# Attending two chunks in a row into the two halves of one bank, and turning their sums' reciprocals together

## What is computed

```python
xq = layer_norm(x, qn_w, qn_b)
ctx = layer_norm(context, cn_w, cn_b)
q = (xq @ q_w).reshape(B, N, H, D)                # B 16, N 256, H 16, D 32
kv = (ctx @ kv_w).reshape(B, M, 2, H, D)
attn = jnp.einsum('bnhd,bmhd->bhnm', q, k) * scale
attn = jnp.where(xa_mask[:, None, :, :], neg, attn)
attn = jax.nn.softmax(attn, axis=-1)
out = jnp.einsum('bhnm,bmhd->bnhd', attn, v).reshape(B, N, C)
x = x + out @ proj_w + proj_b
```

## Time and profile before

| | us |
|---|---|
| median of 3 runs (2743.96 to 2746.96) | 2745.2 |
| the profiled execution, its own time | 2744.09 |
| its span, first to last instruction | 2742.4 |
| PE busy in the span | 2672.3 (97%) |
| DVE busy | 1952.7 (71%) |
| ACT busy | 1558.8 (57%) |
| POOL busy | 734.9 (27%) |
| mean granted PE clock | 0.995 |

### The profile page before, as it was taken

How to read it: one execution, slowest core, us unless ns; L and a number is a source line. 1 busy time by engine, 2 the same in 40 slices (tenths; PEclk the granted TensorE clock), 3 DMA queues, 4 the chain that set the end, 5 groups by cost and what they waited for, 6 DMA issues and landing times.

```text
span 2742.4 us, 68931 instructions
## 1 busy us (share of the span) xinstructions
PE 2672.3 (97%) x24032; PEld 2329.0 (85%) x24032; DVE 1952.7 (71%) x5572; ACT 1558.8 (57%) x4829; POOL 734.9 (27%) x935
## 2 busy tenths in 40 slices
PE   5999999999999999999999999999899999999997
PEld 5888888888888888888889999998788888888886
DVE  6878888887534443445388887887688888888876
ACT  5777777777211111111277777777676766767763
POOL 2333333330000000001013333333233434334343
PEclk9999999999999999999999999999999999999998
DMA  4333333342311211113021111112322212222110
GB/s 152 110 106 97 108 124 102 100 143 86 92 59 34 61 46 46 46 46 100 24 78 46 46 46 46 48 53 73 108 67 69 87 61 75 78 66 95 61 52 19
DMA packets 182230, 202.57 MB, mean 74 GB/s; under 512 B 19344, under 2 KB 109456, under 8 KB 181264
## 3 DMA queue, kind: packets, MB, share of 16 engines
q1 hardware_dynamic: 182160, 201.66, 23.3%
HBM read 137.65 MB, written 63.96 MB: 74 GB/s over the span
## 4 chain that ended last, share of the span: by engine, by line
PE 82%; DVE 8%; ACT 5%; issue 3%; POOL 1%; DMA 1%; SPq 1%; DVEq 0%; ACTq 0%; POOLq 0%
PE mask_work L172 13%; PE mlp_f L3028 13%; PE mlp_acc L3046 13%; PE causal_work L172 9%; PE cross_work L172 9%; PE mask_attended L2079 2%; PE mask_scores L2039 2%; PE mask_probsT L2060 2%; PE mask_scores L2060 2%; PE causal_scores L2039 2%; ACT cross_prob L865 2%; PE cross_probsT L2060 2%; PE causal_attended L2079 2%; PE cross_scores L2039 2%; PE causal_probsT L2060 1%
## 5 line engine op out<-in xcount | busy, mean ns | idle before, releaser
L2824 ACT ACTIVATE mlp_h<-mlp_f,mlp_b1col 128x512 f32<-128x512 f32 x128 | 88.3, 690 | 524.3 <-PE mlp_f L3028 524.3
L3028 PE MATMUL mlp_f<-mlp_xT_hi,mlp_w 128*128 128x512 f32 x1024 | 335.4, 389 | 0.0
L2929 DVE CAST mlp_hT_hi<-mlp_h 128x512 fp32r<-128x512 f32 x128 | 58.2, 454 | 369.8 <-ACT mlp_h L2824 369.7
L3046 PE MATMUL mlp_acc<-mlp_w,mlp_hT_hi 128*128 128x512 f32 x1024 | 315.2, 389 | 0.0
L865 ACT ACTIVATE mask_prob<-mask_scores,mask_low 128x256 f32<-128x256 f32 x512 | 237.7, 485 | 93.5 <-DVE mask_low L1412 93.4
L865 ACT ACTIVATE causal_prob<-causal_scores,causal_low 128x128 f32<-128x128 f32 (+1 forms) x512 | 211.0, 432 | 87.6 <-DVE causal_low L1412 87.6
L865 ACT ACTIVATE cross_prob<-cross_scores,cross_low 128x256 f32<-128x256 f32 x512 | 237.4, 497 | 33.2 <-DVE cross_low L1406 26.1
L1412 DVE CUSTOM_DVE_ANT_0 mask_scores<-mask_scores,mask_mask 128x256 f32<-128x256 f32 x512 | 198.9, 461 | 50.9 <-PE mask_scores L2039 50.3
L3028 PEld LDWEIGHTS mlp_f<-mlp_xT_hi,mlp_w 128*128 128x128 f32 x1024 | 192.1, 188 | 40.6 <-DVE mlp_xT_lo L2915 0.4
L3046 PEld LDWEIGHTS mlp_acc<-mlp_w,mlp_hT_hi 128*128 128x128 f32 x1024 | 192.2, 188 | 39.8
L172 PE MATMUL causal_work<-causal_xT_hi,causal_w 128*128 128x256 f32 x1008 | 221.8, 293 | 1.1 <-DVE causal_qk_parts L1371 1.1
(11 more groups left out here) (349 smaller groups left out, 8236.2 us busy)
## 6 DMA issues: line engine op xcount, KB each, us to landing
cross_x_in<-after_attention SPq DMA_DIRECT2D x17, 512.0 KB, 4.1
mask_x_in<-in_x SPq DMA_DIRECT2D x16, 512.0 KB, 4.5
mask_c_in<-in_ctx SPq DMA_DIRECT2D x16, 512.0 KB, 5.3
mask_res<-in_x SPq DMA_DIRECT2D x16, 512.0 KB, 3.7
after_attention<-mask_res SPq DMA_DIRECT2D x16, 512.0 KB, 2.8
mlp_x<-after_attention SPq DMA_DIRECT2D x8, 1024.0 KB, 5.5
mlp_stage<-in_L_xattn_fc_w SPq DMA_DIRECT2D x8, 1024.0 KB, 5.6
after_layer<-mlp_y SPq DMA_DIRECT2D x8, 1024.0 KB, 4.3
```

Source lines behind the costliest of these rows:

```text
L2824: act.activation(h32[:, m % 2, :], F1[m % 2][:], ACT.Gelu, bias=b1col[:, m:m + 1]).then_inc(s["gelu"], 1)
L3028: ins = pe.matmul(F1[m % 2][:], W[2 * (m // 4)][:, a, k, m % 4 * P:(m % 4 + 1) * P], xT[p][:, k, :], start=(k == 0 and n == 0), stop=(k == ...
L3046: ins = pe.matmul(ACC[t][:], hT[a][:, m % 2, t * P:(t + 1) * P], W[2 * (m // 4) + 1][:, p, m % 4, :], start=(m == 0 and n == 0), stop=(m = ...
```

## The change

In the mask phase the attends of chunks 0 and 1 run one behind the other, behind the scores of chunk 2. Chunk 0 goes to the first half of O and chunk 1 to the second. Those of chunks 2 and 3 run behind the scores of chunk 0 of the next element. ACT copies both halves at once (`pair_kept`, 512 columns), `over_sums` handles two chunks, `turn_sums` makes four transposes that overwrite both halves of O, now behind the transposes of a chunk's second unit, and `normed` multiplies 512 columns, with the semaphore z_ps before it. The four smaller steps per turn become two wider ones. In the loop, the keys of the next element move ahead of the transposes of units 12 and 13. At the phase's end `turn_sums` moves between the halves of the projection. The tiles OT, rs32, sums and rs are laid out for pairs. The other phases keep their form.

```diff
-        OT = r("ot", [P, S])
-        rs32 = r("rs32", [P, TT, HC, DH])
+        OT = r("ot", [P, 2 * S])
+        rs32 = r("rs32", [P, TT, 2 * HC, DH])
...
+        def pair_kept(b, p):
+
+            act.wait_ge(s["av_done"], KC * b + 2 * p + 2)
+            act.activation(OT[:], O[:], ACT.Copy).then_inc(s["ot_done"], 1)
...
-                attended(b, -1)
+                pair_kept(b, -1)
...
-            attended(b, 0)
...
-            attended(b, 1)
+            pair_kept(b, 0)
...
-            attended(b, 2)
...
+        def over_sums(b, p):
+
+            dve.wait_ge(s["exp_done"], UNITS * b + 2 * HC * (p + 1))
+            chain.done(dve.reciprocal(rs[:], sums[:, p]))
+            chain.wait()
+            dve.tensor_copy(rs32[:], rs[:].unsqueeze(3).to_broadcast([P, TT, 2 * HC, DH])).then_inc(s["rs_done"], 1)
+
+        def normed(b, p):
+
+            dve.wait_ge(s["z_ps"], 2 * b + p + 1)
+            at = 2 * (p % 2)
+            dve.tensor_tensor(z32[:, at:at + 2, :], OT[:].rearrange("p (c s) -> p c s", c=2),
+                              O[:].rearrange("p (c s) -> p c s", c=2), ALU.mult).then_inc(s["z_done"], 2)
...
             if prev:
+                normed(b, -1)
                 post_lo(b, 1)
...
-            normed(b, 0)
-            over_sums(b, 1)
             qk_lo(b, 2)
...
-            normed(b, 1)
-            over_sums(b, 2)
+            over_sums(b, 0)
             qk_lo(b, 3)
+            normed(b, 0)
...
-            normed(b, 2)
-            over_sums(b, 3)
+            over_sums(b, 1)
...
+        def turn_sums(b, p):
+
+            pe.wait_ge(s["rs_done"], 2 * b + p + 1)
+            pe.wait_ge(s["ot_done"], 2 * b + p + 1)
+            for i in range(2):
+                for qt in range(TT):
+                    ins = pe.transpose(O[:, i * S + qt * P:i * S + (qt + 1) * P],
+                                       rs32[:, qt, HC * i:HC * (i + 1)].rearrange("p h d -> p (h d)"), ident[:])
+            ins.then_inc(s["z_ps"], 1)
...
         def mask_end(b):
 
-            turn_sums(b, -1)
+            attend(b, -2)
             attend(b, -1)
             yield ROOM
             pe.wait_ge(s["post_lo"], 2 * b - 1)
             project(b, 0, 0)
+            turn_sums(b, -1)
             project(b, 1, 0)
...
             if prev:
-                turn_sums(b, -1)
                 scores(b, 0)
+                attend(b, -2)
                 attend(b, -1)
...
             turn_probs(b, 0)
             turn_probs(b, 1)
+            if prev:
+                turn_sums(b, -1)
...
-            turn_sums(b, 0)
             scores(b, 1)
-            attend(b, 0)
...
-            turn_sums(b, 1)
             if not nxt:
                 yield ROOM
             scores(b, 2)
+            attend(b, 0)
             attend(b, 1)
...
             turn_probs(b, 8)
             turn_probs(b, 9)
+            turn_sums(b, 0)
...
-            turn_sums(b, 2)
             if not nxt:
                 yield ROOM
             scores(b, 3)
-            attend(b, 2)
             if nxt and prev:
                 pe.wait_ge(s["qk_lo"], KC * (b + 1))
                 pe.wait_ge(s["t_lo"], NP * (b + 1) + 2)
                 queries(b + 1, 0)
+                pe.wait_ge(s["t_lo"], NP * (b + 2))
+                keys(b + 1, 0)
             turn_probs(b, 12)
             turn_probs(b, 13)
```

More of the change, by code:

```diff
@@ L235, in attention_phase @@
         m_in = r("m_in", [P, TT, S], U8)
+        OT = r("ot", [P, 2 * S])
+        rs32 = r("rs32", [P, TT, 2 * HC, DH])
         wcol = r("wcol", [P, 4, KC])
-        sums = r("sums", [P, KC, TT, HC])
+        sums = r("sums", [P, KC // 2, TT, 2 * HC])
         low = r("low", [P, 4, TT])
-        rs = r("rs", [P, TT, HC])
+        rs = r("rs", [P, TT, 2 * HC])
         stats = r("stats", [P, 4, 6])
@@ L866, in exps @@
                                      bias=low[:, u % 4, qt:qt + 1], scale=-1.0,
-                                     accum_out=sums[:, c, qt, h:h + 1])
+                                     accum_out=(sums[:, c // 2, qt, HC * (c % 2) + h:HC * (c % 2) + h + 1]
+                                                if masked_ctx else sums[:, c, qt, h:h + 1]))
             ins.then_inc(s["exp_done"], 1)
@@ L1260, in vector @@
     def vector(dve):
-        head = {"mask": 8, "causal": 13, "cross": 14}[kind]
-        per = {"mask": 6, "causal": 17, "cross": 23}[kind]
+        head = {"mask": 6, "causal": 13, "cross": 14}[kind]
+        per = {"mask": 4, "causal": 17, "cross": 23}[kind]
         chain = Chain(dve, s["chain"], head, per)
@@ L1414, in masks_and_minima @@
             ins.then_inc(s["masked"], 1)
-        def over_sums(b, c):
-            dve.wait_ge(s["exp_done"], UNITS * b + HC * (c + 1))
-            chain.done(dve.reciprocal(rs[:], sums[:, c % KC]))
+        def over_sums(b, p):
+            dve.wait_ge(s["exp_done"], UNITS * b + 2 * HC * (p + 1))
+            chain.done(dve.reciprocal(rs[:], sums[:, p]))
             chain.wait()
-            dve.tensor_copy(rs32[:], rs[:].unsqueeze(3).to_broadcast([P, TT, HC, DH])).then_inc(s["rs_done"], 1)
-        def normed(b, c):
-            dve.wait_ge(s["ot_done"], KC * b + c + 1)
-            dve.tensor_tensor(z32[:, c % KC, :], OT[:], O[:, S:2 * S], ALU.mult).then_inc(s["z_done"], 1)
+            dve.tensor_copy(rs32[:], rs[:].unsqueeze(3).to_broadcast([P, TT, 2 * HC, DH])).then_inc(s["rs_done"], 1)
[4 more added lines that the diff above has]
+                              O[:].rearrange("p (c s) -> p c s", c=2), ALU.mult).then_inc(s["z_done"], 2)
         def attended(b, c):
@@ L1538, in mask_turn @@
                 post_lo(b, 0)
-                normed(b, -1)
-            if cur:
-                over_sums(b, 0)
             if cur and prev:
@@ L2072, in attend @@
             pe.wait_ge(s["copied"], UNITS * b + HC * (c + 1))
-            if c in (0, 2):
+            if c % 2 == 0:
                 pe.wait_ge(s["v_ready"], 2 * b + 1 + c // 2)
-            pe.wait_ge(s["z_done"], KC * b + c + 1)
+            at = 0
+            if masked_ctx:
+                if c % 2 == 0:
+                    pe.wait_ge(s["z_done"], KC * b + c + 1)
+                else:
+                    at = S
+            else:
+                pe.wait_ge(s["z_done"], KC * b + c + 1)
             for kt in range(TT):
@@ L2078, in attend @@
                 for h in range(HC):
-                    ins = pe.matmul(O[h * DH:(h + 1) * DH, q0:S], V[:, kt, HC * (c % KC) + h, :],
+                    ins = pe.matmul(O[h * DH:(h + 1) * DH, at + q0:at + S], V[:, kt, HC * (c % KC) + h, :],
                                     probT[:, (HC * c + h) % 8, kt * S:kt * S + S - q0],
@@ L2089, in attended @@
             ins.then_inc(s["z_ps"], 1)
-        def turn_sums(b, c):
-            pe.wait_ge(s["rs_done"], KC * b + c + 1)
-            pe.wait_ge(s["z_done"], KC * b + c + 1)
-            for qt in range(TT):
-                pe.transpose(O[:, S + qt * P:S + (qt + 1) * P], rs32[:, qt].rearrange("p h d -> p (h d)"), ident[:])
+        def turn_sums(b, p):
[6 more added lines that the diff above has]
+            ins.then_inc(s["z_ps"], 1)
         def post_turn(b, p, res=res):
@@ L2276, in mask_turn @@
                 queries(b + 1, 0)
-            if nxt:
                 pe.wait_ge(s["t_lo"], NP * (b + 2))
```

## The result

The changed kernel takes 2755.06 us (median of 6 runs, 2752.37 to 2759.28) where the kernel before takes 2744.98 (6 runs, 2743.58 to 2746.96): a ratio of 1.0041, 95% interval 1.0031 to 1.0051. It is slower by 10.1 us, where 4.5 were forecast; the time lies in the range. The profiled execution spans 2750.6 us against 2742.4, so the traces can show 8.2 of the 10.1.

A forecast was written before the change was run, and what follows sets the result against it. PE bounds the loop (busy 549.88 of 550.40 us). Loop +0.7, turn 0 -0.3, last turn +1.7, end +2.4 sum to +4.5 on 2744.1, 2748.6; with 1.1 for the median 2749.7 us, range 2742 to 2757.

The forecast's parts named there:

- PE's slots: Loop: an attend behind another costs 0.864 us instead of 1.00; each pair saves about 0.12, 0.24 per turn.
- Quarters 1, 2 and 3: Parts of a turn between chunks' first scores: 8.78, 10.79, 8.88 us, with waits for the third unit in 1 and 3.
- The wide copy beside POOL: DVE's 512-column copy of the sums waits for POOL's cast: 0.6 us in quarter 2, 0.43 with POOL idle.
- Quarter 0: Loop, from chunk 0's scores: 10.91 us if the sums' transposes wait for nothing; kept pair ready about +6.6, asked at +6.61.
- rival A: Loop, quarter 0: late DVE minima delay the kept pair behind PE, 0.46 us a turn, +6.4, 2756 us; chance 0.22.
- Last turn: Last turn: quarters 0 and 2 pay 1.08 us each, quarter 1 gains only 0.5, quarter 3 nothing: +1.7 us.
- The end: Phase's end: sums turned behind half a projection, ACT's hi part about 2.8 us later, 0.45 to spare: +2.4 us.
- Rival B: Phase's end: delays hidden by more room in the first gelu's chain or by PE's order, 2746 us; chance 0.12.
- Turn 0: First turn: no sums ahead of scores and a copy less in quarter 1, estimated -0.3 us.
- C: Rival, loop: short quarters don't wait, units ready 0.3 us earlier, 0.60 saved a turn, -8.4, 2741 us; chance 0.08.
- D: Rival, loop: a pair's second attend waits and drains twice, pairs save nothing, +3.4, 2753 us; chance 0.08.

The follow-up runs named there:

- filled paired loop: Changed kernel with half a projection (quarter 1) and half the next values (quarter 3) ahead of the third unit, quarter 0's sums' transposes behind it: 2746.16 us.
- the one with attends apart: Changed kernel, wide steps kept, each attend back behind the next chunk's scores, sums' transposes behind the third unit's: 2744.91 us.
- the extra products: Changed kernel with three products that nothing reads put into PE's waits in turn 0: 2752.25 us; also added to the first joined version: 2742.82 us.
- the early end: Changed kernel with the sums' transposes at the phase's end moved ahead of the projection's first half: 2753.54 us.
- the later sums: Changed kernel with quarter 0's transposes of the sums moved behind the third unit's transposes: 2756.58 us.
- one attend of turn 0 apart: Changed kernel with chunk 0's attend, in turn 0 alone, put back behind the scores of chunk 1: 2754.73 us.
- the first joined version: Changed kernel with the loop's fillings, the end's sums' transposes ahead of the projection, and turn 0's first attend put back: 2743.25 us.
- the keys alone: Kernel before with only the next element's keys moved ahead of the transposes of units 12 and 13: 2740.42 us.
- the longer wait: Kernel before with one of turn 0's four weight conversions on ACT moved ahead of the copy that unit 7 waits for: 2746.22 us.

## Why the prediction was right in its direction and short by half

**PE's slots: right.** A pair starts its next product 1.86 behind itself, forecast 1.00 + 0.864. The saving of 0.24 a turn is what separates the filled paired loop from the one with attends apart (38.83, 39.07). The prediction prices it in two ways, though: 0.12 a pair by the groups, and 1.00 - 0.864 = 0.136 in the quarters' sum, which the measured 1.86 bears out.

**Quarters 1, 2 and 3: right to 0.01** (8.77, 10.79, 8.88 measured; 8.78, 10.79, 8.88 forecast), and each by the reason given: a wait ahead of the third unit in 1 and 3, and none at the sums in quarter 2. Filling quarters 1 and 3 gave 0.26 and 0.24, where the wait with its restart had been put at 0.30.

**The wide copy beside POOL: right.** It was forecast at 0.6 in quarter 2, going by where POOL's cast ends, and at 0.43 with POOL idle. Order of time on POOL and on DVE in quarter 2:

```profile
414.68 1.17 POOL L626 CAST mask_xT_hi<-mask_x_turned 128x512 fp32r<-128x512 f32 x2 [2.98 <-PE mask_work L172]
```

```profile
415.53 0.61 DVE L1425 COPY mask_rs<-mask_rs 128x512 f32<-128x512 f32 x1
```

The copy ends at 416.14, 0.29 after the cast (415.85), and takes 0.43 in quarter 3, where POOL is idle. That agrees with a DVE that waits for POOL's whole instruction, as the Trainium skill states it (SBUF — State Buffer, "Who interferes with whom"). This row alone can't show it: the two overlap for 0.32 only, and a copy at half speed for so long would take 0.43 + 0.16 = 0.59, an estimate as near to the 0.61. It is the longer overlap of the earlier trace rows that speaks for the wait: 0.77 for a copy of 0.29.

**Quarter 0: the step without cover.** The 10.91 held "if the new waits in front of the sums' transposes cost nothing". They cost 0.10 a turn, +1.4 us in 14 turns, at the place where the prediction says "No cover is left here". The minima came when forecast; the kept pair ended at 436.26, q0 + 6.56, and the transposes asked at + 6.62, so the arithmetic even held to 0.01. What the sum had wrong is the hand-over between the two, put at 0.06: from the end of the copy (436.26) to the start on PE (436.41) it is 0.15. Moving the transposes behind the third unit took the wait away (10.89). With a margin of 0.01 the likeliest value should have included part of rival A.

**Last turn: right** (+1.5 for +1.7).

**The end: the mechanism right, the size 0.8 short.** Order of time from the late multiply on, all engines:

```profile
676.44 0.69 DVE L1431 TENSOR_TENSOR mask_z<-mask_ot,mask_attended 128x512 f32<-128x512 f32 x1 [2.54 <-PE mask_attended L2105]
...
677.16 0.63 ACT L910 ACTIVATE mask_zT_hi<-mask_z 128x512 fp32r<-128x512 f32 x1 [4.93 <-DVE mask_z L1431]
...
678.57 0.73 PE L172 MATMUL mask_scores<-mask_w,mask_zT_hi 128*128 128x512 f32 x2 [0.86 <-DVE mask_zT_lo L1493]
...
681.41 0.69 DVE L2943 TENSOR_TENSOR mlp_hT_lo<-mlp_h,mlp_hT_hi 128x512 fp32r<-128x512 f32 x1
...
682.16 0.50 PE L3058 MATMUL mlp_acc<-mlp_w,mlp_hT_hi 128*128 128x512 f32 x1 [0.56 <-DVE mlp_hT_lo L2943]
```

From the hi part's start to the down product is 5.00 (682.16 - 677.16), before it was 5.42: the cover of 0.45 was there, 0.42 of it was used, and PE now waits for the split as forecast. But the hi part comes 17.33 behind the last scores (659.83) where it was 13.77 (667.99 - 654.22), 3.6 later and not 2.8. In this stretch the clock falls, here by window:

```profile
663.60:667.00 3.40, 3.15 (x12) 2.62 (x12) 2.35 (x9) 3.40 (x14) 0.00 (x0) 0.50 0.38 133
```

The kernel with the filled loop has the same end at full clock, and it lasts 21.55 from the last scores on, +2.4, the forecast; its hi part starts 16.56 behind them, the forecast 2.8 later than before. So the missing 0.8 goes with the clock:

```profile
651.30:672.90 21.60, 17.39 (x126) 12.56 (x125) 11.88 (x33) 14.08 (x34) 2.54 (x2) 1.00 0.30 98
```

Rival B, that the ends are hidden, is out.

**Turn 0: wrong in sign, and the largest miss** (+2.3 for -0.3). The step was: "without sums ahead of scores and with a copy less in quarter 1, estimated -0.3". It counted the work of ACT and DVE that sets the turn and nothing for PE's clock, because the trace of before has it at 1.00 there. In all six kernels of the paired order without the extra products that were profiled (the change itself, the early end, the later sums, one attend of turn 0 apart, the filled loop and the first joined version), the clock is at 0.50 somewhere between 49 and 73 us, for 6.8 or 10.2 us in all; with the extra products in turn 0 it is in none of three. Of the four kernels without pairs it isn't in two (the kernel before, and the keys alone), and is in the two that lengthen or thin PE's work there (the longer wait, the wide steps with attends apart). Each was profiled once, so this is a pattern, not a price. With the products and at full clock, turn 0 is 41.09 and 40.89, in versions that have its first attend apart; with the pair in place it is 41.61, and about 40.9 without the 0.7 of the fall near 28 (an estimate, from quarter 0's 10.75 against 10.03). So the order by itself seems to be worth -0.2 to 0, as forecast to a tenth or two.

**The sum.** In the profiled execution: turn 0 2.6 more than forecast, loop 1.3 (2.0 against 0.7), last turn -0.2, end 0.8; the first scores came 0.2 earlier and the rest was 0.5 shorter. That is 3.8 of the 5.6 by which the forecast fell short, and +4.5 becomes +8.3 (8.2 measured). The six runs of the changed kernel range over 6.9 us, with a mean granted clock of 0.993 or 0.994 in the shorter and 0.991 or 0.992 in the two longest, and the profiled one is the shortest. The last 1.9 of the median may be of that kind; no trace shows them, and the late DVE beside POOL of the ends of 24.64 and 24.84 would do as well. That the time lies in the range is in part luck: 2755 was reached in the range's upper part, which was there for rival A, and A's mechanism made 1.4 of it, where the clock made some 3 in the profile. A cause for each fall, and why they vary at unchanged code (near 28 us, ahead of everything that the change touches, in five of the twelve profiled executions behind that of before), stays open.

**The rivals.** C, that the short quarters don't wait, is out: they wait in every turn. It would have been right with the third unit's place filled, and that is what the filled loop does: -0.48 a turn against before. D, that the pairs save nothing, is out by the 0.24. A holds in its mechanism, with 0.10 a turn for its 0.46.

## What to carry to other kernels

Merging two small steps of the bounding engine moves work out of the places where it covered a wait, and the price is read there: ask of each slot that is taken away what PE waits for next, and put other work into it in the same edit (the filled loop gained 0.62 a turn over the change). Split a change into its parts before judging it: here the side effect, keys moved ahead of two units, was worth -0.17% by itself, and the rest cost 0.6% (1.0041 against 0.9983). Where a margin comes out at 0.01 us, count the hand-over and take the late case as the likely one.

## What the runs showed of the hardware

- TensorE's clock fell to half in an opening in which PE waited twice for 2.5 us: turn 0 took 43.37 us at a granted clock of 0.88, and 41.61 with three useless products put into its waits, at 1.00 from 45 us to its end. More work took less time.
- The fall needn't stand behind the wait that was lengthened: 0.52 us more of wait at 50 us was answered by 3.4 us of half clock at 66.1.
- At unchanged code the stretches at half clock came or stayed away from one profiled execution to another: near 28 us in five of twelve. Ends with the same code were 21.55 us with no fall, and 21.87 and 22.34 with one of 3.4 us.
- DVE instructions of 128x512 with two inputs in SBUF took 1.75 and 1.78 us in place of 0.68 where they started while one of POOL's additions ran. Whether they did hung above all on when a DMA landed, 1.1 us apart in two executions of the same code, and the end of the phase took 24.84 us for 22.34.
- Two attends in a row cost less than two apart: 1.86 against 2 x 1.00, and the 0.24 a turn came back in full in the loop's length once nothing else was late.
